# Output bias on GpSimd instead of a matmul, a PE loop of four slots, and new instruction orders in an attention and expert kernel

## What is computed

```
n1 = layernorm(x)
q = n1 @ Wq.T + bq ; k = ctx @ Wk.T + bk ; v = ctx @ Wv.T + bv     (16 heads of 32)
x1 = x + (softmax(q k / sqrt(32)) v) @ Wo.T + bo
n2 = layernorm(x1)
g = softmax(n2 @ W_router.T + b_router), all but the two largest of 8 set to 0
out = x1 + sum over e of g[e] * (n2 @ W_experts[e].T + b_experts[e])
```

## Time and profile before

| | |
|---|---|
| time, median of 3 runs | 1407.37 us (1406.43 to 1410.46) |
| the profiled execution, its own time | 1413.48 us |
| its span, first to last instruction | 1411.8 us |
| PE busy | 1244.1 us (88%), 11616 instructions |
| DVE busy | 856.4 us (61%) |
| ACT busy | 635.4 us (45%) |
| POOL busy | 791.6 us (56%) |
| mean granted clock of PE | 0.935 |
| first matmul of the expert stage | 978.4 us |

### The profile page before, as it was taken

One profiled execution on the slowest core, in us unless ns is written; L12 is line 12 of the kernel. 1 busy time (PEld: TensorE's weight loads), 2 busy tenths in 40 slices (PEclk: granted clock), 3 DMA queues, 4 the chain that ended last, 5 costly groups with the idle time before them and its releaser, 6 DMA issues. The chain is left out here.

```text
span 1411.8 us, 37249 instructions
## 1 busy us (share of the span) xinstructions
PE 1244.1 (88%) x11616; PEld 746.8 (53%) x11617; DVE 856.4 (61%) x1891; ACT 635.4 (45%) x914; POOL 791.6 (56%) x1034
## 2 busy tenths in 40 slices
PE   6596899999899899899899997722899999999997
PEld 3253666656556556566566665411445555555554
DVE  3363787878578678678677766441444544544544
ACT  2114467645645645654654574200333434434433
POOL 3103347677567577667667766662265545544554
PEclk9787799999899999999999998765999999999999
DMA  6624437565555555645645556654689988989986
GB/s 230 190 60 130 129 95 217 139 208 172 147 198 166 166 180 170 197 154 189 184 127 182 179 158 248 224 214 160 120 168 177 173 167 169 180 168 173 171 171 123
DMA packets 135727, 239.05 MB, mean 169 GB/s; under 512 B 18240, under 2 KB 49216, under 8 KB 134464
## 3 DMA queue, kind: packets, MB, share of 16 engines
q1 hardware_dynamic: 101952, 156.99, 36.8%
q0 software_dynamic: 29824, 67.27, 24.2%
q10 hardware_dynamic: 3840, 13.20, 2.5%
HBM read 112.84 MB, written 101.22 MB: 152 GB/s over the span
## 5 line engine op out<-in xcount | busy, mean ns | idle before, releaser
L1794 PE MATMUL Yp<-we_s,gT_hi 128*128 x1088 | 347.9, 381 | 6.4 <-DVE gT_lo L1742 5.7
L1701 POOL DMA_INDIRECT out<-yw,to x136 | 211.1, 1552 | 235.0 <-issue 95.3
L1061 POOL TENSOR_TENSOR we_s<-P_s,we_s 128x1024 f16<-128x1024 f32 x112 | 237.4, 2131 | 75.0 <-ACT we_s L854 58.3
L1794 PE MATMUL Yp<-we_s,gT_lo 128*128 x544 | 207.2, 381 | 0.0
L1718 ACT ACTIVATE gT_hi<-Tp 128x512 f16<-128x512 f32 x138 | 82.3, 596 | 276.0 <-PE Tp L1781 274.2
L1760 DVE SCALAR_TENSOR_TENSOR yb<-Yp,be_s 128x512 f32<-128x512 f32 x136 | 94.1, 692 | 167.6 <-PE Yp L1794 162.5
L903 DVE TENSOR_REDUCE mx_sb<-S 128x6 f32<-128x924 f32 x160 | 171.9, 1114 | 20.5 <-PE S L660 16.2
L643 PE MATMUL W<-we_s,wq_s 128*128 128x512 f16 x512 | 161.5, 393 | 14.1 <-DVE we_s L891 6.0
L1794 PEld LDWEIGHTS Yp<-we_s,gT_hi 128*128 128x128 f16 x1088 | 106.9, 98 | 121.7 <-issue 10.4
L681 PE MATMUL W<-wo_s,aT_hi 128*128 128x512 f16 x512 | 167.9, 390 | 0.0
L1140 POOL DMA_INDIRECT dispatched<-xn,idx x128 | 127.5, 996 | 49.9 <-issue 30.8
(11 more groups left out here) (188 smaller groups left out, 2133.3 us busy)
## 6 DMA issues: line engine op xcount, KB each, us to landing
xg<-dispatched SPq DMA_DIRECT2D x140, 257.0 KB
we_s<-we_s SPq DMA_DIRECT2D x192, 128.0 KB, 2.6
be_s<-in_x SPq DMA_DIRECT2D x16, 1024.0 KB, 6.0
xR_s<-in_x SPq DMA_DIRECT2D x16, 1024.0 KB, 9.4
out<-xR_s SPq DMA_DIRECT2D x16, 1024.0 KB
wst<-in_weT SPq DMA_DIRECT2D x16, 512.0 KB
we_scratch<-wsp SPq DMA_DIRECT2D x16, 512.0 KB, 4.0
we_s<-we_scratch ACTq DMA_DIRECT2D x8, 1024.0 KB, 7.8
```

Of the source, the lines that this page charges most:

```text
L1061: e.tensor_tensor(Pst[1][:, r:r + 2, :], exps(n), Pst[0][:, r:r + 2, :], ALU.subtract).then_inc(pldp, 1)
L1701: e.indirect_dma_start(out, bass.IndirectOffsetOnAxis(ap=to[u][:, :], axis=0), yw[u % YW][:, :], None, bounds_check=N - 1, oob_is_err=Fals ...
L1794: m = e.matmul(Yp[:, u % 2, :], gT[u % 2][xp][:, k, :], we_s[:, bass.ds(n * WN + (wp * KC + k) * D, D)], start=(c == 0), stop=(c == 11))
```

## The change

Three things.

1. The bias matmul of `O` is gone (with `bo_r`, its operand). POOL adds the bias `bo_b` to the loaded residual tokens instead (`pool_BX`, four instructions of 128x512 f32 per block), and `Oe` waits for them.
2. PE's loop body holds four slots: straight code for slots -2 to 3, two turns of slots 4 to 11, straight code for slots 12 to 17. The other engines' loops keep two.
3. All orders are new: the slot lists of every engine, the banks and their holders. PE's slot now starts after `ST0`, and holds steps of `b+2`.

```diff
     def __init__(self, c, reg=None, per=2):
+        self.c, self.reg, self.per = c, reg, per
...
-            if n == 0:
-                e.matmul(W[:, bank, :], ones[:, :], bo_r[:, :], start=True, stop=False)
-            m = e.matmul(W[:, bank, :], aT[ap][:, k, j * P:(j + 1) * P], wo_s[:, wp, k, :], start=False, stop=(n == 11))
+            m = e.matmul(W[:, bank, :], aT[ap][:, k, j * P:(j + 1) * P], wo_s[:, wp, k, :], start=(n == 0), stop=(n == 11))
...
     def dve_Oe(e, b, j):
         e.wait_ge(op_, b.at(4, j + 1))
-        if j == 0:
-            e.wait_ge(ld_xR[b.par], b.half(16, 16))
+        e.wait_ge(p_bx, b.at(NJ, j + 1))
...
+    def pool_BX(e, b):
+        if b.first:
+            e.wait_ge(L["bo"], 48)
+        e.wait_ge(ld_xR[b.par], b.half(16, 16))
+        hold(e)
+        for j in range(NJ):
+            e.tensor_tensor(xR[b.par][:, j, :], xR[b.par][:, j, :], bo_b[:, :], ALU.add).then_inc(p_bx, 1)
...
-    def slots(e, slot, least, most):
+    def slots(e, slot, least, most, per=2):
...
-        n = (NB - most - lo) // 2
+        n = (NB - most - lo) // per
...
-            slot(e, Blk(lo, it))
-            slot(e, Blk(lo + 1, it))
+            for k in range(per):
+                slot(e, Blk(lo + k, it, per))
...
-            slots(e, pe_slot, -2, 1)
+            slots(e, pe_slot, -2, 2, 4)
```

More of the change, by code:

```diff
@@ L58, with __init__ @@
 BANK = {
[4 rows of a table removed]
[4 rows of a table added]
 }
 class Blk:
-    def __init__(self, c, reg=None):
-        self.c, self.reg = c, reg
+    def __init__(self, c, reg=None, per=2):
+        self.c, self.reg, self.per = c, reg, per
     def __add__(self, k):
-        return Blk(self.c + k, self.reg)
+        return Blk(self.c + k, self.reg, self.per)
     @property
@@ L1343, in pe_slot @@
             pe_O(e, bm1, 0, s)
+        if on_bp2:
+            pe_XT(e, bp2, 0, s)
+        if on_bm1:
+            pe_O(e, bm1, 1, s)
+            pe_O(e, bm1, 2, s)
+        if on_b:
+            pe_ST(e, b, 7, s)
+            pe_ST(e, b, 8, s)
         if on_bm2:
             pe_R(e, bm2, s)
+        if on_bp2:
+            pe_XT(e, bp2, 1, s)
+        if on_b:
+            pe_PV(e, b, 2)
+        if on_bp2:
+            pe_XT(e, bp2, 2, s)
+        if on_b:
+            pe_PV(e, b, 3)
+            pe_ST(e, b, 9, s)
+        if on_bm1:
+            pe_O(e, bm1, 3, s)
+            pe_O(e, bm1, 4, s)
+            pe_O(e, bm1, 5, s)
+            pe_O(e, bm1, 6, s)
+        if on_bp1:
+            pe_MX(e, bp1, 0, s)
+            pe_MX(e, bp1, 1, s)
+        if on_bp2:
+            pe_XT(e, bp2, 3, s)
+        if on_bm1:
+            pe_O(e, bm1, 7, s)
+            pe_O(e, bm1, 8, s)
+        if on_bp1:
+            pe_MX(e, bp1, 2, s)
+            pe_MX(e, bp1, 3, s)
+        if on_bm1:
+            pe_O(e, bm1, 9, s)
+        if on_bp2:
+            pe_Q(e, bp2, 0, s)
+        if on_bp1:
+            pe_MX(e, bp1, 4, s)
+        if on_bm1:
+            pe_O(e, bm1, 10, s)
+        if on_bp1:
+            pe_MX(e, bp1, 5, s)
+        if on_bp2:
+            pe_Q(e, bp2, 1, s)
+        if on_bp1:
+            pe_MX(e, bp1, 6, s)
+        if on_bm1:
+            pe_O(e, bm1, 11, s)
+        if on_bp1:
+            pe_MX(e, bp1, 7, s)
+        if on_bp2:
+            pe_Q(e, bp2, 2, s)
+        if on_bp1:
+            pe_MX(e, bp1, 8, s)
+        if on_bp2:
+            pe_Q(e, bp2, 3, s)
+        if on_bp1:
+            pe_MX(e, bp1, 9, s)
+        if on_bp2:
+            pe_Q(e, bp2, 4, s)
+        if on_bp1:
+            pe_MX(e, bp1, 10, s)
+        if on_bp2:
+            pe_Q(e, bp2, 5, s)
+        if on_b:
+            pe_PV(e, b, 4)
+        if on_bp1:
+            pe_MT(e, bp1, s)
+        if on_b:
+            pe_PV(e, b, 5)
+            pe_AT(e, b, 0, s)
+        if on_bm1:
+            pe_LB(e, bm1, s)
+        if on_b:
+            pe_PV(e, b, 6)
+        if on_bp1:
+            pe_ST(e, bp1, 0, s)
     def act_slot(e, s):
@@ L1453, in dve_slot @@
             dve_Ql(e, bp1, 3)
+        if on_bp3 and not bp3.first:
+            dve_norm_var(e, 0, bp3)
         if on_bm1:
             dve_ATl(e, bm1, 1)
-        if on_bm2:
-            dve_RM(e, bm2)
-        if on_bm1:
             dve_ATl(e, bm1, 2)
             dve_ATl(e, bm1, 3)
+        if on_b:
+            dve_WEl(e, b)
         if on_bp1:
@@ L1465, in dve_slot @@
             dve_PL(e, b, 5)
+        if on_bp2:
+            dve_XTl(e, bp2, 0)
+        if on_bm1:
+            dve_Oe(e, bm1, 0)
         if on_bm2:
             dve_RS(e, bm2)
-            dve_RE(e, bm2)
-        if on_bp3 and not bp3.first:
-            dve_norm_var(e, 0, bp3)
-        if on_bm1:
-            dve_Oe(e, bm1, 0)
-        if on_b:
-            dve_WEl(e, b)
         if on_bm1:
             dve_SN(e, bm1, 0)
+        if on_bm2:
+            dve_RE(e, bm2)
         if on_bp2:
-            dve_XTl(e, bp2, 0)
+            dve_XTl(e, bp2, 1)
+            dve_XTl(e, bp2, 2)
         if on_b:
             dve_NM(e, b, 1)
-        if on_bp2:
-            dve_XTl(e, bp2, 1)
         if on_bm2:
@@ L1560, in slots @@
         with e.Fori(0, n) as it:
-            slot(e, Blk(lo, it))
-            slot(e, Blk(lo + 1, it))
-        for s in range(lo + 2 * n, last + 1):
+            for k in range(per):
+                slot(e, Blk(lo + k, it, per))
+        for s in range(lo + per * n, last + 1):
             slot(e, Blk(s))
```

257 lines of the change are left out of this document (91 added, 166 removed), and 8 rows, old and new, of the table BANK.

## The result

The changed kernel takes **1402.34 us** (median of 5 runs, 1398.80 to 1402.86), the kernel before beside it 1409.94 (5 runs, 1406.43 to 1411.34). The ratio is 0.9922 with an interval of 0.9900 to 0.9944: 8 us faster, where 24 were predicted. 1402 lies in the given range, and almost on the rival "the clock falls in part", 1403.

The account below looks back on a forecast made before the run. The prediction took PE to set the attention stage's pace, POOL not far behind. Terms -14 -21 -2 -30 +43 gave -24 us: a span of 1388, a median of 1384 us; 8-in-10 range 1345 to 1412.

Parts of the forecast that it names:

- the clock falls in part: Rival: PE's clock drops to 1.2 GHz at the new waits, half covered or every other block; +19, 1403 us, chance 0.2.
- The two waits: PE waits for POOL at PV0 (1.8 us) and PV2 (1.7 to 1.8 us): 3.6 us in twelve blocks, +43.
- The old waits: PE's small waits in a block, 3.0 us, shrink by 2.5 under the new orders: -30 in twelve blocks.
- The forecast 0.45: Chance 0.45 given to the prediction's own sum, 1384 us, with its own range 1372 to 1396.
- A mis-sized term: `BX`: POOL's bias additions, 1.05 us each (ends 0.8 and 1.25), four per block ahead of PL3 and PL4, behind PV2's wait.
- the meeting: POOL's `BX` running into DVE's `WEl`: priced at 0.7 us per block; by the port rule up to 1.25.
- The loop: PE's loop of four slots: three returns fewer at 7 us each, -21; the one left partly covered, -2.
- The bias matmul: -14: 64 bias matmuls of 0.22 us leave PE, the engine taken to set the pace: -14 us.
- the second wait: PE at PV2 waits for POOL's PL4, 1.7 to 1.8 us; 0.8 or 2.6 with the ends of `BX`.

Follow-up runs that it names:

- f2: The kernel before, unchanged, run with a profile in the second kind of set: 1385.84 us, 0.9994 of the kernel before.
- f1: The changed kernel, unchanged, run with a profile in the second kind of set: 1399.48 us, 1.0089 of the kernel before.
- f3: The kernel before with PE's loop of four slots and nothing else: 1373.78 us, 0.9905 of the kernel before.
- e1: The changed kernel with PE's loop back to two slots: 1399.67 us, 1.0067 of the kernel before.
- e2: The changed kernel with the bias matmul back and no `BX` on POOL: 1381.34 us, 0.9937 of the kernel before.
- g4: The same program as f3, run again in a set with the pauses: 1394.66 us, 0.9868 of the kernel before.
- g1: The kernel before with the loop of four, no bias matmul, and `BX` on POOL behind `NA` and PL7, old orders: 1395.53 us, 0.9867 of the kernel before.
- i1: h1 without `BX`, the output bias left out altogether, in a set with the pauses: 1394.37 us, 0.9853 of the kernel before.
- h1: The kernel before with the loop of four, no bias matmul, and `BX` behind `NA` and PL4, old orders: 1398.47 us, 1.0084 of the kernel before.
- h3: h2 with the bias matmul made twice, the first overwritten: 1376.92 us, 0.9930 of the kernel before.
- h4: h2 with eight overwritten matmuls of 32 columns ahead of each bias matmul: 1383.86 us, 0.9981 of the kernel before.
- e4: The changed kernel with POOL's second scatter `SD` moved behind PL7 of the same slot: 1389.87 us, 1.0007 of the kernel before.
- h2: The same program as f3 and g4, the kernel before with the loop of four, in another set: 1370.34 us, 0.9879 of the kernel before.

## Why the prediction was wrong

**What held.** The two waits stood where they were forecast. PE reached PV0 and PV2 and waited there for PL1 and PL4: 1.76 and 2.1 us, predicted 1.8 and 1.7 to 1.8. Over 300 to 840 us that is 33.9 us of idle time in twenty pieces, 37 by the 0.16 us that each piece is longer; 3.6 us in eleven blocks would be 40. **The old waits** went: 19.7 us (7.2, 6.3, 4.9 and 1.3) became 2.4, which with 0.16 for each of the 40 pieces that went is 24, predicted 27.5 for eleven blocks. But three quarters of them exist in one kind of set only: in f2 there are just those at the router's bank.

**The step that failed: "The forecast 0.45; ... the clock falling in part 0.2 (1403)".** The sum has no term for the clock, which was left to a rival. It should have had one: the clock falls in each of the ten blocks. Where it falls behind PV2, in five of them, the block is 1.2 to 1.5 us longer than the 48.9 of f1's blocks without a fall, 6.7 us together; behind PV0 it costs next to nothing. The evidence was in the earlier trace rows, where the clock fell around a wait of 2.04 us, and in the earlier trace rows; against it stood only that waits of 0.4 to 0.5 us left it at 1.00 in the earlier trace rows. Waits of 1.8 us are nearer to the first. An unknown price is to be taken from the row that it is nearest to; the prediction did that for `BX`, and not here. The rival's mechanism and place were right. That its +19 meets the measured time is luck: the clock gives 7 us in the ten blocks, as much as a mis-sized `BX` does, and 5 come from how the median was set (both below).

**A mis-sized term: `BX`.** Taken at 1.05 us each and 4.9 with the meeting; it is 1.23 by starts (the upper end was 1.25), and 5.95 with the meeting, since that costs 1.07 and not 0.7. The estimate from the Trainium skill (GPSIMD Engine Reference, on elementwise work), 1.12 us, is nearer than my row but low as well. PE's wait at PV2 is only 0.3 us longer than forecast, as PE itself gets there 0.4 later; what counts is that PV2 starts 27.2 us behind `MT` instead of 26.4. From there to the next `MT` PE takes 21.7 us at full clock, and 21.8 were forecast, so a block has 48.9 us where the prediction's terms give 48.2.

**The loop.** A return at the old place costs 6.5 to 6.8 us in f2, near the 7 taken, but the loop alone gives only 13 to 17 us and not 21 (f3). In the new orders a return costs nothing (e1), so it was the place that removed the returns' cost, not the number; the changed kernel's one return is in a block 1 us longer than the others and 2.2 longer than 48.9, where I had left 5. The term was right in size for the whole change and had the wrong owner.

**The bias matmul: -14.** No run shows that it paid. At full clock a block of the changed kernel is POOL's part, from `MT` to PV2, and PE's, from PV2 to the next `MT`. By PE's list one of the four bias matmuls stood in the first part, where PE waits anyway, and three in the second. What replaced them, `BX`, lengthens the first by more: e2, with the matmul and without `BX`, has blocks of 47.5. The prediction's own terms already made this part of the change a loss, and it didn't say so: 14 us saved, against the second wait, twelve times 1.75 us, which only `BX` creates. In the old orders the pauses take the gain in one kind of set (g4 against g1, i1), and in the other POOL's ring costs more than that (h1). That kind of set has no run of the old orders with neither the bias matmul nor `BX`; h3 suggests some 0.8 us per block.

**What is left.** In the ten blocks 498.1 us were measured. The earlier trace rows give 508.0; less 8.8, 23 and 25, plus 36, by the prediction's terms for ten blocks, that is 487. The 11 missing are: 7 of the clock; 7 since a block has 48.9 and not 48.2; 1.6 of pauses in two blocks; less 3, as the return costs 2.2 and not 5; less 1.6 in the last block, which takes 47.3. Outside the ten blocks the prediction's terms give 3 us less than before, and the traces 1 less: the head of the kernel, up to the first `MT`, is 5 us shorter (105.2, before 110.6), which nobody predicted; from the last `MT` to the end the changed kernel loses 3, 2 of them in the expert stage, where the code is the same. That makes 13 us in the profiled span (1401.0 against 1388). The other 5 of the 18 between 1384 and 1402 are no mechanism: the prediction set the median 6 us below the profiled execution, as it was before, and the changed kernel's profiled execution is 0.5 above its median.

Not settled: why PE and VectorE pause in some sets and not in others (instructions arriving late there is possible; h3 and h4 were run only where there are no pauses), and what makes the clock fall behind a wait of 1.8 us in one block and not in the next. The length of the wait alone doesn't decide it: in f1 pairs of waits of 1.6 and 2.2 us left it at 1.00 in four blocks, in e4 waits of 2.7 us and more did in seven, and in h2 it fell behind 0.4 to 0.6.

## What to carry to other kernels

Before work is moved from the busiest engine to one that has a quarter of its time free, follow that engine's list around the ring: what is added anywhere in it arrives at the first result that another engine waits for, one slot later if need be. A wait of PE of 1.5 to 2 us can cost more than itself, because the clock may fall behind it (here 1.2 to 1.5 us more where PE's own work follows, and next to nothing where a later wait for another engine takes it up); put that into the sum by the nearest row. Split a block at the places where PE waits, and ask of each saving in which part it lies. Try the parts of a change one by one: here the plain loop of four slots in the old orders beats the whole change by 8 to 26 us.

## What the hardware showed that I had not expected

The same program takes 1387 us in one set of runs and 1410 to 1418 in another, by pauses of 0.4 to 1.2 us at the same place of each block, while a kernel whose PE waits for POOL anyway takes 1399 to 1402 in both. GpSimd's f32 addition of 512 columns takes 1.27 us alone and up to 2.34 us when a VectorE instruction on 1024 columns meets it; moved apart, it is never above 1.295. PE's clock fell for 3.4 us behind waits of 1.5 to 2.2 us in nine of the changed kernel's ten blocks, in about half of them in f1, behind two of nine waits of 2.7 to 3.1 us in e4, and in h2 also in blocks whose longest wait was 0.6; with four matmuls more in the block (h3) it didn't, but for the return.
